# New places in the written order of an attention and feed-forward kernel

## The chip, the cores and the metric

One core of a Trainium2 chip. The metric is the device time of one execution in microseconds. The kernel before was run three times; its median is 1648.62 us (1646.54 to 1649.3). One more execution was taken with the profiler on: it took 1646.02 us, of which 1644.1 us lie between its first and its last instruction (the span of the trace).

## The reference, cut to what matters

```
q   = rms_norm(x @ w_qa.T) @ w_qb.T         # 16 heads, 128 + 64 channels
q_pe = q_pe * cos + rotate_half(q_pe) * sin # the 64 rope channels of each head
c, k_pe = x @ w_kva.T                       # one latent key of 128, one rope key of 64
scores = q_full @ k_full.T * scale          # causal, 2048 x 2048 per head
out = softmax(scores) @ v
x = layernorm(x + out @ w_o.T)
x = layernorm(x + (x @ (weight * scale).T + bias))
```

All is float32. The kernel writes each float32 operand of a matmul as a rounded high part and a rest ("hi" and "lo") and adds the products of the parts.

## The kernel before, in words

A first phase (up to about 150 us) makes keys, values and split weights. Then come attention, the output projection and the feed-forward layer in one long program of single steps.

**Tiles.** The 16 heads are taken in 4 groups of 4. In a group the kernel goes over the 16 query tiles of 128 tokens, two at a time (a pair). One query tile of one group is an iteration `it` (64 of them), and one iteration has one step for each key tile `t` up to the diagonal, `keys(it)` of them. In all there are 544 tiles (iteration, key tile), each 128 keys by 4 heads by 128 queries. The last four iterations have 4, 3, 2 and 1 tiles.

**One tile** goes this way: TensorE makes the scores with five products (L1475) in one of three banks. For `t > 0` ScalarE copies them to a ring of 24 buffers (L1592) and VectorE takes the running maximum (L1849); for `t = 0` VectorE adds the mask (L1839). Later VectorE subtracts the maximum (`shift`, L1880), ScalarE takes the exponential (`exp`, L1597) and rounds it (`hi`, L1604), VectorE sums it (`sum`, L1887), GpSimd forms the rest (`lo`, L1708). TensorE then adds two products with the high part and one with the rest to the bank `OUT` (`values`, L1493, L1494, L1496). `hi` of a tile waits for the value products two tiles before, since `split_p` has two halves.

**One iteration** also has: the maximum over keys (`reduce_max` L1857 on VectorE, `widen_max` L1718 on GpSimd, `fold_max` L1484 on TensorE, `join_max` L1864 and `spread_max` L1872 on VectorE), the same for the sum (`reduce_sum` L1895, `fold_sum` L1505, `spread_sum` L1901 and L1903, `normalise` L1910), `copy_out` (L1610, ScalarE takes `OUT` to `o_sum`; the next iteration's first value product waits for it), `o_hi` (L1616, ScalarE), `o_lo` (L1725, GpSimd), the projection `y` (12 products, L1517; the last four wait for `o_lo`) and `add_y` (L1828). `copy_out` of `it` waits for `o_lo` of `it - 2`.

**One pair** has two projections `q` (18 products each, L1438) with `q_hi` (L1575, ScalarE) and `q_lo` (L1821, VectorE), and one projection `pe` (18 products, L1451). Its result is turned by rope: `rope` on VectorE (three multiplications, L1800 and twice L1804), then on GpSimd one subtraction and one addition (`rotate`, L1681 twice), a rounding on ScalarE (`round_pe`, L1579), the rest on GpSimd (`rest`, L1687), a store to memory and a load in another layout on the SP queue (`store_pe`, `load_pe`).

**The last block** (`ffn`) takes the 16 sums of the last group through layer norm, turn, linear layer and layer norm: units `u` from 0 to 15, with `statistics` (L1929), `centre` (L1623, ScalarE), `invert` (GpSimd), `turn` (L1525, TensorE), `copy_x` (L1640, ScalarE), `rest_x` (L1915, VectorE), `scale` (L1634), `add_bias` (L1747), `linear` (12 products, L1537), `z` (L1946), `z_statistics` (L1952), `z_invert` (GpSimd), `apply` (L1644), `out`.

**What sets the order.** Every engine runs its own steps in the order of one list, `STEPS`. It is made by `plan()`: every step has a place, a number of slots times 13 plus a constant of the table `AT`; the steps are sorted by place; and a step that another one needs (`waits_for`) is put in before it, if it isn't there yet. So a step whose own place is later than that of one that needs it goes where the other goes. Scores of tile number n have place 13 n - 2. The value slot v of a tile is at least 6 slots behind the last scores of its iteration; `shift`, `exp`, `hi`, `sum`, `lo` and `values` are placed from 13 v, the steps of an iteration from its last score slot or its last value slot. Below, 123@10 means slot 123, 10 thirteenths. Three banks `AUX` are shared in turn by `q`, `pe`, `y`, `fold_max`, `fold_sum`, `turn` and `linear`; each waits until the third use before it has been read.

In the kernel before, GpSimd's `rotate` runs at the step `rope`, as does VectorE's `rope`, and the units of the last block have slots 543, 545, ... 567, 570, 572, 574.

Of the kernel before, what the change touches and what calls it, by code (L numbers as in the profile page):

```python
# [742 lines left out]

SPREAD, SCORES_AT, COPIES, SHIFT, EXP, ROUND, VALUES, READ, MAX, USE_AT, FFN_TURN, FFN_LINEAR, FFN = range(13)

W_SLOT = FIRST[N_ITER - 4] + 3
DIRECT = NT - 2
PACE = 2
# [7 lines left out]
def ffn_slots():  # L756

    slots = []
    for u in range(NT):
        ready = last_value(output_of(u)) + (9 if u < DIRECT else 7)  # L760
        if u == 2:
            ready = max(ready, N_TILE)
        slots.append(max(slots[-1] + PACE if slots else W_SLOT + 6, ready))
    return slots
# [5 lines left out]
AT = {'scores': -2, 'max': 7.85, 'shift': -36, 'exp': -22, 'hi': -14, 'sum': -7.75, 'lo': -7.65, 'values': 1, 'reduce_max': 19, 'widen_max': 24, 'fold_max': 38, 'join_max': 46, 'spread_max': -26, 'reduce_sum': 1, 'copy_out': 10, 'fold_sum': 46, 'spread_sum': 38, 'normalise': 33.1, 'o_hi': 51, 'o_lo': 49.25, 'y': 76, 'add_y': 60.15, 'q': 9, 'q_hi': 45.85, 'q_lo': 19.95, 'pe': 6, 'rope': 19.85, 'round_pe': 63, 'store_pe': 58, 'load_pe': 66}  # L770


def timetable():

    for it in range(N_ITER):
        for t in range(keys(it)):
# [3 lines left out]
            for what in ("shift", "exp", "hi", "sum", "lo", "values"):  # L780
                yield 13 * v + AT[what], 0, (what, it, t)
        for what in ("reduce_max", "widen_max", "fold_max", "join_max"):
            yield 13 * last_slot(it) + AT[what], 0, (what, it)
# [3 lines left out]
    for s in range(-2, N_PAIR):  # L787
# [3 lines left out]
        for j, use in enumerate(uses):  # L791
# [7 lines left out]
            if use[0] == "pe":  # L799
                yield 13 * at + AT["rope"], 0, ("rope", s + 2)  # L800
                yield 13 * at + AT["round_pe"], 0, ("round_pe", s + 2)
# [4 lines left out]
def ffn_timetable():  # L806
# [3 lines left out]
    for u in range(NT):  # L810
        n = FFN_SLOT[u]
        if u < DIRECT:
            yield n - 3, FFN, ("in", u)
        yield n + 0, SPREAD, ("statistics", u)
        yield n + 0, ROUND, ("centre", u)
        yield n + 1, FFN, ("invert", u)
        yield n + 1, FFN_TURN, ("turn", u)
        yield n + 2, READ, ("copy_x", u)
        yield n + 2, READ, ("rest_x", u)
        yield n + 2, FFN, ("scale", u)  # L820
        yield n + 3, FFN, ("add_bias", u)
        yield n + 4, FFN_LINEAR, ("linear", u)
        yield n + 5, READ, ("z", u)
        yield n + 5, MAX, ("z_statistics", u)
# [1241 lines left out]
```

## Time and profile before

| | before |
|---|---|
| median of three runs | 1648.62 us (1646.54 to 1649.3) |
| profiled execution | 1646.02 us |
| its span | 1644.1 us |
| outside the span | 1.9 us |
| TensorE busy | 1596.1 us, 97% |
| TensorE weight load busy | 1326.8 us, 81% |
| VectorE busy | 1452.7 us, 88% |
| ScalarE busy | 1117.5 us, 68% |
| GpSimd busy | 992.7 us, 60% |

Shares are of the span. The matmuls of TensorE overlap and their ends are modelled, so "busy" says that one was recorded as under way, not that the array was full. PE is TensorE, PEld its weight load, DVE VectorE, ACT ScalarE, POOL GpSimd.

### The profile page before, as it was taken

The page shows a single profiled execution, that of the slowest core. Times are in us where ns is not written, and L with a number is a line of the kernel's source. Part 1 is how long each engine was busy: PE and PEld are TensorE (multiplying, and loading weights), DVE is VectorE, ACT ScalarE, POOL GpSimd, SP SyncE. Part 2 cuts the span into 40 slices and gives each one's busy share as a digit, 9 for nine tenths or more (in the row PEclk, how much of TensorE's full clock was granted, in tenths as well). Part 3 has the DMA queues.
Part 4 walks back from the last instruction along what each step waited for, and adds up shares of the span by engine and source line. Part 5 has one row for each costly group of instructions (what it writes and reads, how often), then busy time and mean ns, then how long its engine had stood idle before and what let it go on. Part 6 is the DMA issues. An engine that isn't in the chain of part 4 may idle for free.

```text
span 1644.1 us, 26779 instructions
## 1 busy us (share of the span) xinstructions
PE 1596.1 (97%) x8021; PEld 1326.8 (81%) x8021; DVE 1452.7 (88%) x2688; ACT 1117.5 (68%) x2064; POOL 992.7 (60%) x1001
## 2 busy tenths in 40 slices
PE   7999999999999999999999999999999999999887
PEld 5568888878888878878888878788888888888665
DVE  3656899999999999989999899999999999999995
ACT  3554676666777666766777666766767777776674
POOL 4333566665666666666666566566656666666785
PEclk9999999999999999999999999999999999999999
DMA  7994322212321412223212422123123111112322
GB/s 212 364 358 132 115 79 65 91 58 77 130 84 39 142 45 84 71 84 129 84 58 76 122 67 84 39 83 132 60 75 116 46 64 59 52 46 83 106 94 84
DMA packets 112168, 163.93 MB, mean 100 GB/s; under 512 B 13600, under 2 KB 83488, under 8 KB 109984
## 3 DMA queue, kind: packets, MB, share of 16 engines
q1 hardware_dynamic: 105296, 125.86, 23.7%
q10 hardware_dynamic: 1872, 20.19, 3.0%
q0 software_dynamic: 4864, 16.26, 3.0%
q8 instruction: 62, 1.02, 0.3%
q14 instruction: 74, 0.61, 0.1%
HBM read 101.19 MB, written 61.08 MB: 99 GB/s over the span
## 4 chain that ended last, share of the span: by engine, by line
PE 78%; DVE 11%; issue 4%; POOL 3%; DMA 2%; ACT 2%; DVEq 0%; ACTq 0%; SPq 0%; POOLq 0%
PE rows L1475 21%; PE bank L1475 11%; PE rows L1517 8%; PE bank L1496 6%; PE bank L1493 6%; PE bank L1494 6%; PE rows L1438 5%; PE bank L1438 4%; DVE parts L1887 3%; PE bank L1517 2%; DVE top L1849 2%; PE bank L1451 2%; PE rows L392 2%; DMA cq_dram<-cq 2%; DVE bank L1872 1%
## 5 line engine op out<-in xcount | busy, mean ns | idle before, releaser
L1708 POOL TENSOR_TENSOR split_p<-pool,split_p 128x512 fp32r<-128x512 f32 x544 | 702.6, 1297 | 348.3 <-ACT split_p L1604 347.6
L1604 ACT CAST split_p<-pool 128x512 fp32r<-128x512 f32 x544 | 338.4, 622 | 99.7 <-PE bank L1496 70.0
L1887 DVE TRANSPOSE_TENSOR_REDUCE parts<-pool 128x16 f32<-128x512 f32 x544 | 379.3, 697 | 0.2
L1880 DVE TENSOR_TENSOR pool<-bank,pool 128x512 f32<-128x512 f32 x544 | 369.4, 679 | 2.2
L1597 ACT ACTIVATE pool<-pool 128x512 f32<-128x512 f32 x544 | 342.4, 629 | 32.8 <-DVE pool L1880 29.4
L1475 PE MATMUL rows<-q_c,key_c 128*128 128x512 f32 x1089 | 311.4, 394 | 0.0
L1592 ACT COPY pool<-rows 128x512 f32<-128x512 f32 x320 | 186.9, 584 | 123.4 <-PE rows L1475 123.4
L1493 PE MATMUL bank<-split_p,val 128*128 128x512 f32 x544 | 219.6, 404 | 9.9 <-ACT o_sum L1610 9.9
L1475 PEld LDWEIGHTS rows<-q_c,key_c 128*128 128x128 f32 x1089 | 198.2, 189 | 35.7
L1475 PE MATMUL rows<-q_pe,key_pe 128*128 128x512 f32 x726 | 225.1, 391 | 0.0
L1496 PE MATMUL bank<-split_p,val 128*128 128x512 f32 x544 | 214.8, 395 | 2.9 <-POOL split_p L1708 2.6
L1494 PE MATMUL bank<-split_p,val 128*128 128x512 f32 x544 | 213.2, 392 | 0.0
L1849 DVE TENSOR_TENSOR top<-rows,top 128x512 f32<-128x512 f32 x283 | 188.9, 668 | 15.8 <-ACT pool L1592 15.3
L1475 PEld LDWEIGHTS rows<-q_pe,key_pe 128*128 128x128 f32 x726 | 136.6, 188 | 29.6
L1517 PE MATMUL rows<-wo,o_t 128*128 128x512 f32 x600 | 146.6, 392 | 8.2 <-POOL o_t L1725 6.1
L1475 PE MATMUL bank<-q_c,key_c 128*128 128x512 f32 x543 | 154.4, 392 | 0.0
L1517 PEld LDWEIGHTS rows<-wo,o_t 128*128 128x128 f32 x600 | 112.5, 189 | 33.8 <-POOL o_t L1725 7.3
L1592 ACT COPY pool<-bank 128x512 f32<-128x512 f32 x160 | 93.4, 584 | 65.6 <-PE bank L1475 65.6
L1493 PEld LDWEIGHTS bank<-split_p,val 128*128 128x128 f32 x544 | 102.8, 189 | 31.8 <-ACT o_sum L1610 12.6
L1496 PEld LDWEIGHTS bank<-split_p,val 128*128 128x128 f32 x544 | 102.6, 189 | 29.7 <-POOL split_p L1708 8.5
L1494 PEld LDWEIGHTS bank<-split_p,val 128*128 128x128 f32 x544 | 102.9, 189 | 18.8
L1475 PEld LDWEIGHTS bank<-q_c,key_c 128*128 128x128 f32 x543 | 99.4, 189 | 18.6
(200 smaller groups left out, 2378.4 us busy)
## 6 DMA issues: line engine op xcount, KB each, us to landing
q_pe<-pe_dram SPq DMA_DIRECT2D x128, 128.0 KB, 2.6
y_dram<-y SPq DMA_DIRECT2D x62, 256.0 KB, 2.1
cq<-cq_dram SPq DMA_DIRECT2D x19, 768.0 KB, 4.8
y<-y_dram SPq DMA_DIRECT2D x48, 256.0 KB, 3.4
pe_dram<-by_sin SPq DMA_DIRECT2D x32, 256.0 KB, 2.1
pe_dram<-by_cos SPq DMA_DIRECT2D x32, 256.0 KB, 2.1
cq_more<-cq_dram SPq DMA_DIRECT2D x10, 768.0 KB, 5.0
table<-table_dram SPq DMA_DIRECT2D x56, 128.0 KB, 2.7
```

The costliest lines, as they stand in the source:

```text
L1475: mm = pe.matmul(by_head(out), k, q, start=(z == 0), stop=(z == 4))
L1493: pe.matmul(OUT, m.val[:, 0, j, :], split_p[:, n % 2, 0, :], start=(t == 0), stop=False)
L1494: pe.matmul(OUT, m.val[:, 1, j, :], split_p[:, n % 2, 0, :], start=False, stop=False)
L1496: pe.matmul(OUT, m.val[:, 0, j, :], split_p[:, n % 2, 1, :], start=False, stop=(t == keys(it) - 1)).then_inc(values_done, 1)
L1517: mm = pe.matmul(aux(u), o_t[:, a, h * P:h * P + P], m.wo[:, b, h, :], start=(n == 0), stop=(n == 3 * HG - 1))
L1592: nc.scalar.copy(slot(n), SCORES[n % N_SCORES]).then_inc(scores_copied, 1)
L1597: nc.scalar.activation(slot(n), slot(n), ACT.Exp).then_inc(exp_done, 1)
L1604: nc.scalar.copy(split_p[:, n % 2, 0, :], slot(n)).then_inc(p_hi, 1)
L1708: nc.gpsimd.tensor_tensor(split_p[:, n % 2, 1, :], slot(n), stored(split_p[:, n % 2, 0, :]), ALU.subtract).then_inc(p_lo, 1)
L1849: nc.vector.tensor_tensor(out, SCORES[n % N_SCORES], slot(number(it, 0)) if t == 1 else out, ALU.max).then_inc(scores_maxed, 1)
L1880: nc.vector.tensor_tensor(slot(n), MAXES, slot(n), ALU.add).then_inc(shifted, 1)
L1887: nc.vector.tensor_reduce(parts[:, t, :], in_blocks(slot(n)), AX.X, ALU.add, apply_transpose=True).then_inc(summed, 1)
```

## The change

The change alters places and one condition; no instruction is added or taken away.

- `rotate` becomes a step of its own. It needs `rope`, and `round_pe` needs `rotate`. GpSimd runs its subtraction and addition at this step and no longer at `rope`. Its place is `13 * at + 11.9`, where `pe` has `13 * at + 6`; `rope` has 16.85 (it had 19.85).
- The value products of an iteration's first tile have the place 13 v + 10, those of the others 13 v + 1 as before.
- Other places: `shift` -36 to -35, `exp` -22 to -20, `sum` -7.75 to -5.6, `lo` -7.65 to -15.65, `reduce_sum` 1 to -5, `copy_out` 10 to 10.15, `o_hi` 51 to 44, `q_lo` 19.95 to 19.8, `store_pe` 58 to 55.
- The steps of the last block take their places from the same table, in thirteenths, and many move by a few; the block's units get slots 542, 544, ... 572.

```diff
+AT = {'scores': -2, 'max': 7.85, 'shift': -35, 'exp': -20, 'hi': -14, 'sum': -5.6, 'lo': -15.65, 'values': 1, 'reduce_max': 19, 'widen_max': 24, 'fold_max': 38, 'join_max': 46, 'spread_max': -26, 'reduce_sum': -5, 'copy_out': 10.15, 'fold_sum': 46, 'spread_sum': 38, 'normalise': 33.1, 'o_hi': 44, 'o_lo': 49.25, 'y': 76, 'add_y': 60.15, 'q': 9, 'q_hi': 45.85, 'q_lo': 19.8, 'pe': 6, 'rope': 16.85, 'round_pe': 63, 'store_pe': 55, 'load_pe': 66, 'f_in': -27, 'f_statistics': 0, 'f_centre': 6, 'f_invert': 17, 'f_turn': 25, 'f_copy_x': 30, 'f_rest_x': 30.05, 'f_scale': 46, 'f_add_bias': 51, 'f_linear': 63, 'f_z': 70, 'f_z_statistics': 72.85, 'f_z_invert': 85, 'f_apply': 101, 'f_out': 106.05, 'f_ready': -4, 'f_ready_last': 7, 'f_pace': 2, 'f_first': 3, 'w_slot': 5, 'rotate': 11.9, 'values_first': 10.0}
...
-W_SLOT = FIRST[N_ITER - 4] + 3
+W_SLOT = FIRST[N_ITER - 4] + AT["w_slot"]
 DIRECT = NT - 2
-PACE = 2
+PACE = AT["f_pace"]
...
-        ready = last_value(output_of(u)) + (9 if u < DIRECT else 7)
+        ready = last_value(output_of(u)) + (AT["f_ready"] if u < DIRECT else AT["f_ready_last"])
...
-        slots.append(max(slots[-1] + PACE if slots else W_SLOT + 6, ready))
+        slots.append(max(slots[-1] + PACE if slots else W_SLOT + AT["f_first"], ready))
...
-AT = {'scores': -2, 'max': 7.85, 'shift': -36, 'exp': -22, 'hi': -14, 'sum': -7.75, 'lo': -7.65, 'values': 1, 'reduce_max': 19, 'widen_max': 24, 'fold_max': 38, 'join_max': 46, 'spread_max': -26, 'reduce_sum': 1, 'copy_out': 10, 'fold_sum': 46, 'spread_sum': 38, 'normalise': 33.1, 'o_hi': 51, 'o_lo': 49.25, 'y': 76, 'add_y': 60.15, 'q': 9, 'q_hi': 45.85, 'q_lo': 19.95, 'pe': 6, 'rope': 19.85, 'round_pe': 63, 'store_pe': 58, 'load_pe': 66}
...
-            for what in ("shift", "exp", "hi", "sum", "lo", "values"):
+            for what in ("shift", "exp", "hi", "sum", "lo"):
                 yield 13 * v + AT[what], 0, (what, it, t)
+            yield 13 * v + AT["values" if t else "values_first"], 0, ("values", it, t)
...
                 yield 13 * at + AT["rope"], 0, ("rope", s + 2)
+                yield 13 * at + AT["rotate"], 0, ("rotate", s + 2)
...
-        yield n + 0, SPREAD, ("statistics", u)
-        yield n + 0, ROUND, ("centre", u)
...
+        for what in ("in", "statistics", "centre", "invert", "turn", "copy_x", "rest_x", "scale", "add_bias", "linear", "z",
+                     "z_statistics", "z_invert", "apply", "out"):
+            if what != "in" or u < DIRECT:
+                yield n + AT["f_" + what] / 13, 0, (what, u)
...
     elif what == "round_pe":
+        yield ("rotate", it)
+    elif what == "rotate":
         yield ("rope", it)
...
-                elif what == "rope":
+                elif what == "rotate":
                     rotate(*at)
```

## Rows read from the trace of the kernel before

**Rows 1.** The page's first two parts: span, then busy us of each engine.
```profile
span 1644.1 us, 26779 instructions
...
PE 1596.1 (97%) x8021; PEld 1326.8 (81%) x8021; DVE 1452.7 (88%) x2688; ACT 1117.5 (68%) x2064; POOL 992.7 (60%) x1001
```

**Rows 2.** The chain that ended last: start us, us, engine, line.
```profile
168.32 2.27 PE rows L1475 x10
...
255.38 2.15 PE rows L1451 x18
259.62 2.73 PE rows L1517 x12
```

**Rows 3.** Windows: busy us of each engine by stretch, then granted clock and DMA.
```profile
180.00:300.00 120.00, 118.65 (x606) 101.02 (x605) 112.03 (x196) 83.85 (x151) 73.67 (x66) 1.00 0.22 71
300.00:1500.00 1200.00, 1189.45 (x5972) 1009.03 (x5971) 1120.57 (x1948) 850.97 (x1529) 750.40 (x651) 1.00 0.24 79
1528.00:1545.00 17.00, 12.61 (x48) 9.93 (x47) 15.70 (x35) 11.57 (x20) 11.94 (x17) 0.80 0.04 14
1545.00:1590.00 45.00, 39.27 (x180) 30.32 (x179) 42.81 (x96) 31.23 (x55) 40.79 (x70) 1.00 0.31 100
1590.00:1620.00 30.00, 26.67 (x124) 21.50 (x125) 22.69 (x51) 16.26 (x28) 21.62 (x42) 1.00 0.29 97
```

**Rows 4.** TensorE's waits, 180 to 1500 us: total us, times, longest us.
```profile
PE rows L1517 <- POOL o_t L1725: 6.1, 3, 2.0
PE bank L1493 <- ACT o_sum L1610: 4.2, 4, 1.2
PE bank L1496 <- POOL split_p L1708: 1.0, 1, 1.0
```

**Rows 5.** Timeline around 605 us: start, us, engine, line, [idle before].
```profile
606.25 0.50 PE L1493 MATMUL bank<-split_p,val 128*128 128x512 f32 x1 [1.17 <-ACT o_sum L1610]
...
607.05 2.31 PE L1451 MATMUL bank<-cq,wq 128*128 128x256 f32 x18
```

**Rows 6.** Timeline, 342 to 348 us.
```profile
342.58 0.68 DVE L1880 TENSOR_TENSOR pool<-bank,pool 128x512 f32<-128x512 f32 x1
...
343.18 0.70 DVE L1887 TRANSPOSE_TENSOR_REDUCE parts<-pool 128x16 f32<-128x512 f32 x1
...
343.80 0.65 DVE L1800 TENSOR_TENSOR by_cos<-rows,table 128x512 f32<-128x512 f32 x1
...
344.38 0.74 DVE L1804 TENSOR_TENSOR by_sin<-rows,table 128x256 f32<-128x256 f32 x2
...
345.20 1.42 POOL L1681 TENSOR_TENSOR by_cos<-by_cos,by_sin 128x256 f32<-128x256 f32 x2 [5.02 <-DVE by_sin L1804]
...
346.58 1.27 POOL L1725 TENSOR_TENSOR o_t<-o_sum,o_t 128x512 fp32r<-128x512 f32 x1
...
347.90 1.19 PE L1517 MATMUL rows<-wo,o_t 128*128 128x512 f32 x4 [2.03 <-POOL o_t L1725]
```

**Rows 7.** TensorE's waits, 1500 to 1645 us.
```profile
PE bank L1493 <- ACT o_sum L1610: 5.7, 3, 2.2
PE rows L1484 <- DVE x_t L1915: 2.2, 1, 2.2
...
PE rows L1525 <- ACT x_in L1623: 0.3, 1, 0.3
```

**Rows 8.** Timeline of the last block's first and last units.
```profile
1530.40 0.72 ACT L1623 ACTIVATE x_in<-x_in,ffn_small 128x512 f32<-128x512 f32 x1 [1.37 <-DVE ffn_small L1935]
...
1531.03 0.56 ACT L1610 COPY o_sum<-bank 128x512 f32<-128x512 f32 x1
...
1626.05 3.06 PE L1537 MATMUL rows<-w_t,x_t 128*128 128x512 f32 x12 [1.01 <-DVE x_t L1915]
```

**Rows 9.** The page's costliest groups: GpSimd's rest and ScalarE's rounding of one tile.
```profile
L1708 POOL TENSOR_TENSOR split_p<-pool,split_p 128x512 fp32r<-128x512 f32 x544 | 702.6, 1297 | 348.3 <-ACT split_p L1604 347.6
L1604 ACT CAST split_p<-pool 128x512 fp32r<-128x512 f32 x544 | 338.4, 622 | 99.7 <-PE bank L1496 70.0
```

More of the change, by code:

```diff
@@ L811, in ffn_timetable @@
         n = FFN_SLOT[u]
-        if u < DIRECT:
-            yield n - 3, FFN, ("in", u)
-        yield n + 0, SPREAD, ("statistics", u)
-        yield n + 0, ROUND, ("centre", u)
[L816 to L824, printed above, removed]
-        yield n + 6, READ, ("z_invert", u)
-        yield n + 8, COPIES, ("apply", u)
-        yield n + 8, COPIES, ("out", u)
+        for what in ("in", "statistics", "centre", "invert", "turn", "copy_x", "rest_x", "scale", "add_bias", "linear", "z",
+                     "z_statistics", "z_invert", "apply", "out"):
+            if what != "in" or u < DIRECT:
+                yield n + AT["f_" + what] / 13, 0, (what, u)
 def readers(use):
```

## The prediction

> **What bounds the kernel now.** I read the page first. TensorE is busy for 97% of the span, VectorE for 88% [rows 1]. Busy matmul time has modelled ends, so next comes the chain that ended last: back to back, ten score products take 2.27 us, 18 projection products 2.15 us and 12 output products 2.73 us, so a 512-column product costs 0.227 us [rows 2]. Then the windows: from 180 to 1500 us TensorE is busy for 118.65 + 1189.45 = 1308.1 of 1320 us, so it stands idle for 11.9 us there, and VectorE is busy for 112.0 + 1120.6 = 1232.6 us, 93% [rows 3]. TensorE bounds this stretch and VectorE is close behind. TensorE's waits say what the 11.9 us are: 6.1 us in three waits of the output projection for GpSimd's `o_lo`, 4.2 us in four waits of a first value product for `copy_out`, 1.0 us in one wait for `lo` [rows 4]. No wait for a score bank, for `q_lo` or for `fold_max` stands among them. Nothing that only shifts work on another engine inside that stretch can give more than these 11.9 us.
>
> After 1528 us it is another kernel: the last block on top of the last values. VectorE is busy for 15.7 of 17 us, then for 42.8 of 45 us: with 3.5 us idle in 62 it bounds this stretch. TensorE has 10 us idle there. From 1590 us on neither is full (26.7 and 22.7 of 30 us) [rows 3], and short dependencies set the time.
>
> A sentence of the Trainium skill (Perfetto Trace Analysis, Identifying the Most-Contended Engine) speaks against this reading: it has matmul busy time as a bad measure and asks for the share of weight loads, which is 84% here (1009 of 1200 us). By it TensorE would have up to 16% to spare, VectorE would be the bound and the middle's 6.5 us below would be 0. The trace does not bear it out as a gap: ten products in 2.27 us leave no room for an eleventh.
>
> **The change, part by part.** No instruction comes or goes, so all terms are waits.
>
> *First value product.* At 13 v + 10 it passes only what lies between v@1 and v@10 on TensorE: a `pe` (at @6), a `fold_sum` (@7), a `y` (@8, pulled there by `add_y`) or a `q` (@9). In the other slots nothing changes on TensorE. I compared the slots of the first products with those of the projections: 15 of the 64 have one of these in the same slot before the scores end. All four waits of the middle are among them. At 606.25 the product waited 1.17 us for `copy_out` and the 2.31 us of `pe` came right behind [rows 5]; now `pe` goes first and `copy_out` is done before it ends. The next iteration's wait, at 611.5 us, gets a whole `y` of 2.73 us [rows 2] in front. The pattern comes again one group later. Gain: all of 4.2 us [rows 4].
>
> *Rotation.* `rotate` has the place 11.9 and needs `rope` (16.85), so it pulls `rope` up to 11.9: the new 16.85 has no effect. `rope` was at slot r+1@6.85 and is at r@11.9. On VectorE it passes `shift` and `sum` of the next slot. On GpSimd `rotate` keeps its neighbours, since `lo` moves 8 thirteenths up as well and `o_lo` stays. What it buys is seen at 342 us: `shift` 342.58, `sum` 343.18, `rope` 343.80; GpSimd's `rotate` waits 5.02 us for it, holds `o_lo` behind it, and TensorE stands for 2.03 us in the middle of `y` [rows 6]. Passing both gives 343.80 - 342.58 = 1.22 us. But `normalise`, `join_max`, `reduce_max` and `q_lo` now pass `sum` (@7.4 instead of @5.25), and a `normalise` two steps ahead of this `rope` puts that `sum` in its way: 0.62 us back. Net 0.6 us each, and the pattern comes three times: 1.8 of the 6.1 us [rows 4]. Bounds: nothing (if the `sum` costs more) and 3 x 1.22 = 3.7 us.
>
> What waits behind it: `rope` needs the `pe` product, which until now had `shift` and `sum` in front as cover, 0.68 + 0.70 us [rows 6]. Without cover VectorE can stand up to 1.4 us more for each of 30 ropes, at most 41 us of the 87 us that it has idle in the middle. Behind it are `shift`, then `exp`, `hi`, `lo` of a tile whose value slot is three slots on, with at least three score groups of 1.14 us in between, and the maximum that frees a score bank, of which there are three. As no wait for either stands in rows 4, I take 0. The memory side stays: `store_pe` is three thirteenths earlier on SP, passes no transfer, and `load_pe` keeps its place; no wait of TensorE for it is in rows 4. `q_lo` loses up to one `sum` of cover in the same way and is taken at 0.
>
> *`lo`, `hi`, `exp`, `shift`, `sum`, `reduce_sum`, `copy_out`, `o_hi`.* On GpSimd `lo` passes only `widen_max`, which is then 1.30 us later but no longer blocks a `lo` that is ready. `hi` is pulled along and keeps its place behind `copy_out`. `o_hi` and `round_pe` pass `exp`; where `o_hi` has to wait, `exp` is now behind it, about 0.6 us, the length of one rounding [rows 9], which the ring of 24 hides. All 0, except the 1.0 us of the very first values, of which I take half (bounds 0 and 1.0) [rows 4].
>
> *The last block.* Its first slot goes from 543 to 542, its last from 574 to 572. `statistics` and `centre` of unit 0 come a slot earlier, so `centre` (0.72 us at 1530.40) no longer stands in front of `copy_out` (1531.03) [rows 8], for which TensorE waited 2.2 us [rows 7]; and `copy_x` passes the next `centre`, which frees the bank for which `fold_max` waited 2.2 us. VectorE bounds this stretch, though: its idle time up to 1545 us is 1.3 us, and I take that (bounds 0 and the 3.5 us up to 1590 us) [rows 3]. From 1590 to 1620 us a first product that waited for `copy_out` gets `turn` and `y` in front; another (slot 564) loses `linear` in front and keeps only `turn`. Of the two I keep 0.8 us (bounds -1.5 and +3.3, TensorE's idle time there). At the end the distance of units 12 and 13 falls from three slots to two and `copy_x` is ahead of `centre`, so the waits of 1.01 us [rows 8] and 0.3 us before it [rows 7] go: 1.3 us. The chain behind the last `linear` stays. In all 3.4 us.
>
> *The clock.* Between 1528 and 1545 us the granted clock is 0.80 on the mean [rows 3], that is 6.8 us at 1.2 GHz instead of 2.4, which costs TensorE 3.4 us; it fell right after the two waits of 2.2 us. I count 0, as VectorE bounds there. By the Trainium skill (TensorE: Matmul & The Clock Gate, Part 1: The HAM clock gate) the gate follows how busy the array has been of late, and so shorter waits would give these 3.4 us back; the trace agrees in the order of events, though not every such wait of the middle was followed by a fall.
>
> **Sum.** 4.2 + 1.8 + 0.5 + 3.4 = 9.9 us. The profiled execution goes from 1646.0 to 1636.1 us. It lies 2.6 us under the median of the runs, so I forecast 1638.7 us, 0.6% less. A difference of 0.2% (3.3 us) is about what a measurement can tell from none.
>
> **Rivals.**
> - *Only the middle gives (chance 0.17).* The last block is bound by VectorE, its earlier start only queues more work behind the same engine: 6.5 us, 1642.1 us. For it: VectorE is busy for 42.8 of 45 us from 1545 us on [rows 3]. Against it: the loose end behind 1590 us.
> - *More comes back (0.13).* All 11.9 us of the middle, the 3.5 us of VectorE up to 1590 us and 2 us at the end: 17.4 us, 1631.2 us. For it: `o_lo` needs to be only 2 us earlier. Against it: the `sum` in front of `rope`.
> - *No change (0.10).* Uncovered `rope` and `q_lo` stand so long that VectorE, at 93%, becomes the bound of the middle; the 87 us idle are eaten up in places, the gain is paid back: about 1648 us. The skill's sentence above, that TensorE is not the bound, would end here too.
> - *Slower (0.12).* The loop `values` to `hi` to `lo` to `values` two tiles on. Between the end of a first product and the third tile's last product TensorE has two score groups (2.27 us), one tile of products (0.68) and two more (0.46): 3.4 us. The loop needs 0.62 + 1.30 us [rows 9] and three hand-overs of about 0.08 us (`rope` ends at 345.12, `rotate` starts at 345.20 [rows 6]): 2.1 to 2.2 us. A late first product takes away what stood in between as reserve (up to 2.7 us). If two more ScalarE steps of 0.6 us [rows 9] and a `rotate` of 1.42 us [rows 6] all get in the way, it needs 4.7 us: 1.3 us of wait at 15 places, 20 us, less the 9.9 us won: about 1659 us. It decides from 0.66 us a place on. Against it: the engines are free for more than a third of the time.
> - The forecast's own case, 1634 to 1641 us, has 0.48.
>
> **How the numbers follow.** The range takes the forecast, the first two rivals and the edge of the third: 1630 to 1647.5 us leaves out 0.2, most of it on the slow side. Faster by over 0.2% (under 1645.3): 0.48 + 0.17 + 0.13 = 0.78. Within 0.2%: 0.10. Slower: 0.12.
>
> **What would show it.** In the profile after: no wait of L1493 for `copy_out` in the middle; three waits of L1517 for `o_t` near 346, 702 and 1058 us, each of about 1.4 us; TensorE's idle time from 180 to 1500 us about 5.5 us; L1800 right behind a maximum (L1849 or L1839) and waiting for L1451 in more places than now; a granted clock above 0.80 behind 1525 us. The prediction is wrong if TensorE waits at L1496 for `lo` in many places, if L1475 waits for a maximum, or if the stretch behind 1500 us is longer than now.

## The result: 1.1% faster, by more than was forecast

| | before | after |
|---|---|---|
| median of 5 runs each, same chip | 1648.15 us (1646.54 to 1649.3) | 1629.64 us (1629.43 to 1631.57) |
| profiled execution | 1646.02 us | 1629.54 us |
| its span | 1644.1 us | 1627.6 us |

The ratio is 0.9887, with an interval from 0.9876 to 0.9898. The medians are 18.5 us apart, the profiled executions 16.5 us. The forecast was 1638.7 us, 9.9 us less in the profiled execution, with a range from 1630 to 1647.5 us. The time lies 0.4 us outside the range, on the fast side. Of the 2 us between 16.5 and 18.5 the traces show nothing: the median before lies 2.1 us over its profiled execution, that of after 0.1 us. What follows is about the 16.5 us.

Line numbers of the changed kernel are 7 smaller in all steps: L1493 is L1486, L1517 is L1510, L1800 is L1793. The page of the changed kernel, to be held against [rows 1]:

```profile
span 1627.6 us, 26779 instructions
...
PE 1589.9 (98%) x8021; PEld 1326.2 (81%) x8021; DVE 1445.9 (89%) x2688; ACT 1110.2 (68%) x2064; POOL 995.4 (61%) x1001
```

The instructions are the same in number; only waits went. The windows of the changed kernel (columns as in [rows 3]):

```profile
180.00:300.00 120.00, 120.00 (x615) 102.53 (x614) 112.64 (x199) 85.45 (x155) 75.85 (x69) 1.00 0.22 71
300.00:1500.00 1200.00, 1193.97 (x6019) 1016.85 (x6018) 1124.52 (x1962) 850.04 (x1539) 758.50 (x655) 1.00 0.25 80
1518.00:1535.00 17.00, 12.50 (x48) 9.71 (x47) 16.07 (x35) 11.77 (x21) 12.50 (x19) 0.80 0.01 2
1535.00:1580.00 45.00, 40.37 (x188) 31.32 (x187) 42.89 (x97) 34.88 (x60) 41.16 (x72) 1.00 0.31 100
1580.00:1610.00 30.00, 28.41 (x133) 22.82 (x131) 23.43 (x58) 16.20 (x27) 22.15 (x42) 1.00 0.33 106
```

TensorE's idle time between 180 and 1500 us fell from 11.9 us [rows 3] to 6.0 us. The waits of the changed kernel's TensorE in that stretch:

```profile
PE rows L1510 <- POOL o_t L1718: 4.3, 3, 1.4
PE rows L1444 <- DMA wq<-wq_dram: 1.7, 3, 1.0
```

Against [rows 4], all four waits for `copy_out` and the one for `lo` are gone, the three for `o_lo` are 1.4 us long each in place of 2.0, and one kind is new: the projection `pe` waits three times, once for each new group of heads, for its weights (`wq`).

Idle time is not the whole of it. I put the two traces beside each other step by step, with the first scores at zero, and noted at which tile number the changed kernel gets ahead. It is 10.5 us ahead when the scores end:

| where (tile number of the scores) | ahead by, us | in the forecast |
|---|---|---|
| 187 and 188, 323 and 324: first value products | 1.44 + 1.23 + 1.42 + 1.27 = 5.4 | 4.2 |
| 86, 222, 358: `y` behind `o_lo` | 3 x 0.59 = 1.8 | 1.8 |
| 22: the very first values | 1.2 | 0.5 |
| 359: a fall of the granted clock that does not come | 1.55 | 0 |
| 50: a `y` waits less for `o_hi` | 0.5 | 0 |
| four places of a third of a us, others under 0.2 | about 2.4 | 0 |
| 113, 249, 385: `pe` waits for the weights of the next group | -0.47 - 0.62 - 1.17 = -2.3 | 0 |

The last block gives 5.1 us more: the last `linear` starts 15.6 us ahead. The chain behind it is 0.8 us shorter. Of the 5.1 us about 1.5 are won in the first 62 us behind the last scores, where the windows above and [rows 3] end their second stretch (1590 us before, 1580 us after), and 3.6 behind them: counted off instruction by instruction from the last scores, TensorE is 1.5 us ahead at 55 us and 1.9 at 70, VectorE 1.5 at 62 and at 70.

### The profile page after: what moved, and what is told of

It reads as the page before. It is cut to its first block, busy times and chain, and to the rows that moved or that the text cites. A ratio compares the mean times of both kernels' runs of the same rounds, so it can differ in the third digit from the quotient of the medians.

```text
span 1627.6 us, 26779 instructions
## 1 busy us (share of the span) xinstructions
PE 1589.9 (98%) x8021; PEld 1326.2 (81%) x8021; DVE 1445.9 (89%) x2688; ACT 1110.2 (68%) x2064; POOL 995.4 (61%) x1001
## 4 chain that ended last, share of the span: by engine, by line
PE 89%; POOL 3%; DMA 3%; DVE 2%; issue 1%; ACT 1%; DVEq 0%; ACTq 0%; SPq 0%; POOLq 0%
PE rows L1468 25%; PE bank L1468 12%; PE rows L1510 8%; PE bank L1486 7%; PE bank L1489 7%; PE bank L1487 7%; PE rows L1431 5%; PE bank L1431 4%; PE bank L1510 3%; PE bank L1444 2%; PE rows L392 2%; PE rows L1444 2%; DMA wq<-wq_dram 2%; PE rows L1530 1%; POOL split_p L1701 1%
## 5 line engine op out<-in xcount | busy, mean ns | idle before, releaser
L1486 PE MATMUL bank<-split_p,val 128*128 128x512 f32 x544 | 218.5, 402 | 1.3 <-ACT o_sum L1603 1.3
L1510 PE MATMUL rows<-wo,o_t 128*128 128x512 f32 x564 | 136.9, 391 | 4.3 <-POOL o_t L1718 4.3
L1510 PEld LDWEIGHTS rows<-wo,o_t 128*128 128x128 f32 x564 | 105.4, 188 | 27.5 <-POOL o_t L1718 5.6
L1486 PEld LDWEIGHTS bank<-split_p,val 128*128 128x128 f32 x544 | 102.6, 189 | 21.3 <-ACT o_sum L1603 2.2
```

Source lines behind the costliest of these rows:

```text
L1486: pe.matmul(OUT, m.val[:, 0, j, :], split_p[:, n % 2, 0, :], start=(t == 0), stop=False)
L1510: mm = pe.matmul(aux(u), o_t[:, a, h * P:h * P + P], m.wo[:, b, h, :], start=(n == 0), stop=(n == 3 * HG - 1))
```

## What the changed places look like

The timeline of the changed kernel's TensorE at the place of [rows 5]:

```profile
602.35 2.32 PE L1444 MATMUL bank<-cq,wq 128*128 128x256 f32 x18
...
604.50 0.40 PE L1486 MATMUL bank<-split_p,val 128*128 128x512 f32 x1
...
606.48 2.99 PE L1510 MATMUL rows<-wo,o_t 128*128 128x512 f32 x12
609.31 0.39 PE L1486 MATMUL bank<-split_p,val 128*128 128x512 f32 x1
```

`pe` now runs ahead of the first product, which no longer stands, and the next iteration's first product has the whole `y` in front. And at the place of [rows 6]:

```profile
340.67 0.65 DVE L1842 TENSOR_TENSOR top<-bank,top 128x512 f32<-128x512 f32 x1
...
341.25 0.67 DVE L1793 TENSOR_TENSOR by_cos<-rows,table 128x512 f32<-128x512 f32 x1
...
341.85 0.74 DVE L1797 TENSOR_TENSOR by_sin<-rows,table 128x256 f32<-128x256 f32 x2
...
342.66 1.43 POOL L1674 TENSOR_TENSOR by_cos<-by_cos,by_sin 128x256 f32<-128x256 f32 x2 [4.43 <-DVE by_sin L1797]
...
344.06 1.26 POOL L1718 TENSOR_TENSOR o_t<-o_sum,o_t 128x512 fp32r<-128x512 f32 x1
...
345.37 1.19 PE L1510 MATMUL rows<-wo,o_t 128*128 128x512 f32 x4 [1.43 <-POOL o_t L1718]
```

`rope` comes right behind a maximum, as foretold. `rotate` still stands first in GpSimd's queue, 4.43 us in place of 5.02, and still holds `o_lo` behind it: the wait of `y` is 0.6 us shorter, not gone.

At the end of the program TensorE's waits in the changed kernel, from 1500 to 1645 us, are these (before: [rows 7]):

```profile
PE bank L1489 <- POOL split_p L1701: 3.7, 4, 1.2
PE bank L1477 <- POOL wide_max L1711: 2.0, 1, 2.0
PE bank L1510 <- ACT o_t L1609: 1.3, 2, 0.9
PE bank L1486 <- ACT o_sum L1603: 1.3, 1, 1.3
```

`copy_out` cost 5.7 us in three waits and costs 1.3 us in one. The place of the 2.2 us that `fold_max` waited for `rest_x` is taken by 2.0 us for `widen_max`. In the first 62 us behind the last scores TensorE's waits are as long as before, 9.1 us for 9.4. Behind them they fall from 5.3 to 1.8 us. Two that went stood for VectorE's `rest_x`, and VectorE there stood for ScalarE's `copy_x`. From 1590 to 1633 us before:

```profile
PE bank L1537 <- DVE x_t L1915: 1.5, 1, 1.5
PE rows L1537 <- DVE x_t L1915: 1.0, 1, 1.0
```

```profile
DVE x_t L1915 <- ACT x_t L1640: 6.6, 6, 2.0
```

From 1580 to 1618 us after:

```profile
DVE x_t L1908 <- ACT x_t L1633: 1.0, 1, 1.0
```

What moved most is not on TensorE. ScalarE's largest wait between 1515 and 1650 us is `centre` for VectorE's `statistics`; first before, then after:

```profile
ACT x_in L1623 <- DVE ffn_small L1935: 23.3, 15, 4.2
```

```profile
ACT x_in L1616 <- DVE ffn_small L1928: 11.0, 11, 2.0
```

## The experiments

All change only values of the table `AT`. Kernels called "undone" start from the changed kernel, kernels called "alone" from the kernel before, which the new code gives back when every value is set to its old one. "Middle" is what the step by step comparison gives from the first scores to the last, "end" what it gives behind them; both in us of the profiled executions. One execution each stands behind these figures: `u_inv`, which changes nothing in the middle, is 1.5 us later there at its first tile, and such a step is in the middle of `u_tile` and `u_lo` too (1.2 and 1.6 us).

The theories on trial: that each part's gain is its own and adds up, as my sum has it; that the parts carry each other; and, for the end, which part of it gives more than the 3.4 us that I allowed.

### u_first: first value product undone

```diff
-'values_first': 10.0
+'values_first': 1.0
```

> The changed kernel with the first value product back at 13 v + 1. Theory A (first products win what stood before them): the middle loses 5.4 us again, in two steps of 1.4 and 1.3 us near score tiles 187/188 and 323/324, with four waits of L1486 for copy_out. Theory B (the gain at these tiles came from copy_out itself being earlier, through o_hi and lo): the middle loses under 1 us. Whole kernel by A about 1635 us, by B 1630 us; behind 1500 us at most 2 us either way.

1637.3 us, ratio to before 0.9938 (0.9921 to 0.9954). Against the changed kernel 5.65 us later in the middle and 1.4 us at the end. The waits of its TensorE from 150 to 1500 us:

```profile
PE bank L1486 <- ACT o_sum L1603: 5.7, 7, 1.2
```

Here are seven waits where the kernel before has four. At tiles 90, 226 and 362 three new ones of 1.21 us came, at the place behind which the wait for the weights had been: 0.47 + 0.62 + 1.17 us of that are not paid here, since `pe` runs behind the first tile's value products again. The four places of the forecast lose 4.1 us of the 5.4 that they had won; that the middle as a whole comes near the 5.4 us expected is luck (3 x 1.21 lost, 2.3 won back). At 187 and 323 the step was 1.42 and 1.44 us where the waits read were 1.15 and 1.17 us:

```profile
605.30 0.51 PE L1486 MATMUL bank<-split_p,val 128*128 128x512 f32 x1 [1.15 <-ACT o_sum L1603]
```

So a stop costs some 0.27 us more than the idle time on record (1.42 - 1.15).

### u_rope: rope and rotate undone

```diff
-'rope': 16.85, 'rotate': 11.9
+'rope': 19.85, 'rotate': 19.85
```

> The changed kernel with rope and rotate back at 19.85. Theory A (rope passes shift and sum): the three waits for o_lo grow from 1.4 to at least 2.0 us each, the clock falls again near the third one and takes 1.6 us, and the middle loses 3.4 to 5 us: about 1634 us. Theory B (the three steps of 0.6 us came from lo, sum and o_hi): it loses under 1 us. Since sum now stands in front of the maximum and behind normalise, the waits could even be 2.6 us each.

1636.25 us, 0.9929 (0.9912 to 0.9945). Middle 5.1 us later, end 0.2. Its waits in the middle:

```profile
PE rows L1510 <- POOL o_t L1718: 6.1, 3, 2.0
```

The waits for `o_lo` of [rows 4] are back to the number. 1.8 of the 5.1 us are the steps at 86, 222 and 358; the first values cost 0.6, and two falls of the granted clock, at 703 and 1058 us, both right behind a wait for `o_lo`, cost 3.1 us.

### u_tile: shift, exp, sum, lo, the copies, q_lo and store_pe undone

```diff
-'shift': -35, 'exp': -20, 'sum': -5.6, 'lo': -15.65, 'reduce_sum': -5, 'copy_out': 10.15, 'o_hi': 44, 'q_lo': 19.8, 'store_pe': 55
+'shift': -36, 'exp': -22, 'sum': -7.75, 'lo': -7.65, 'reduce_sum': 1, 'copy_out': 10, 'o_hi': 51, 'q_lo': 19.95, 'store_pe': 58
```

> The changed kernel with shift, exp, sum, lo, reduce_sum, copy_out, o_hi, q_lo and store_pe back at their places of before. Theory A (these hardly matter in the middle): it loses the 1.2 us at the very first values and nothing else there, and the o_lo waits get shorter by 0.6 us each since sum hides again in front of normalise: the middle within 1 us of the changed kernel, about 1630 us. Theory B (the earlier lo carries the gain): TensorE waits at L1489 or L1510 in several places, 5 us or more.

1662.04 us, 1.0089 (1.0071 to 1.0107): slower than the kernel before, 32.2 us worse in the middle. I had all of these at 0.

```profile
PE bank L1489 <- POOL split_p L1701: 22.1, 23, 2.9
```

`values` waits 23 times for `lo`. The parts are not independent.

### u_lo: the place of lo alone undone

```diff
-'lo': -15.65
+'lo': -7.65
```

> The changed kernel with lo alone back at -7.65. Undoing nine places cost 32 us. Theory A (it is lo alone: rotate at r@11.9 now stands in front of lo of tile r+2 at r+1@5.35 and holds it): the same, 1660 to 1664 us, with some 20 waits of L1489 for lo, each after a rotate. Theory B (exp, shift and sum carry it): under 10 us, below 1640 us.

1673.55 us, 1.0152 (1.0135 to 1.0169): 49 us worse in the middle, the most costly single value of the change. The profiled execution was the slowest of four; between the medians it is 44 us. First its TensorE's largest wait from 180 to 1500 us, then GpSimd's for `rope` in that stretch:

```profile
PE bank L1489 <- POOL split_p L1701: 32.0, 38, 3.5
```

```profile
POOL by_cos L1674 <- DVE by_sin L1797: 112.0, 29, 6.2
```

One of the 29, in its timeline:

```profile
344.09 0.62 ACT L1597 CAST split_p<-pool 128x512 fp32r<-128x512 f32 x1
...
350.52 1.41 POOL L1674 TENSOR_TENSOR by_cos<-by_cos,by_sin 128x256 f32<-128x256 f32 x2 [6.22 <-DVE by_sin L1797]
...
351.89 1.26 POOL L1701 TENSOR_TENSOR split_p<-pool,split_p 128x512 fp32r<-128x512 f32 x1
...
353.21 0.79 PE L1489 MATMUL bank<-split_p,val 128*128 128x512 f32 x1 [3.46 <-POOL split_p L1701]
353.80 5.32 PE L1510 MATMUL rows<-wo,o_t 128*128 128x512 f32 x12
```

`rotate` stands at the head of GpSimd's queue for 6.22 us, waiting for `rope`. The `lo` behind it, whose `hi` was done at 344.71 us, doesn't run until 351.89 us, although GpSimd has nothing else to do, and `values` stands for 3.46 us. The 12 products of `y` then take 5.32 us in place of 2.73 [rows 2]: they run at the lower clock. In the changed kernel `lo` is placed eight thirteenths up and so ahead of `rotate`.

### a_lo: the place of lo alone, on the kernel before

```diff
-'lo': -7.65
+'lo': -15.65
```

> The kernel before with lo at -15.65 alone, rope and rotate at 19.85. Theory A (lo alone only lifts the first wait and passes widen_max): 1.2 us less near tile 22, the three o_lo waits of 2.0 us as before, 1646 to 1647 us. Theory B (lo ahead of rotate is the gain, and rope's move adds little): 5 us or more less, below 1643 us.

1647.93 us, 1.0 (0.999 to 1.001); the profiled executions differ by 0.1 us. The 1.2 us near tile 22 did not come. The waits of [rows 4] are all there, to the tenth but for 4.1 in place of 4.2. By itself the place of `lo` is worth nothing; it is what makes `rotate` bearable at its new one.

### a_lorope: lo, rope and rotate alone

```diff
-'lo': -7.65, 'rope': 19.85, 'rotate': 19.85
+'lo': -15.65, 'rope': 16.85, 'rotate': 11.9
```

> The kernel before with rope and rotate at 11.9 and lo at -15.65; sum stays at -7.75, in front of normalise. Theory A (lo keeps its neighbours, rope passes shift and sum): the first values win 1.2 us, the three o_lo waits fall by 1.2 us each to about 0.8 us, the fall of the clock at the third one may go (1.6 us): 1641.5 to 1643.5 us. Theory B (sum in front hurts rope): no less than 1646 us.

1638.53 us, 0.9948 (0.9932 to 0.9965): 8.3 us better in the middle, 0.3 worse at the end. `y` wins 1.16 us at each of 86, 222 and 358, twice what it wins in the whole change, because `sum` keeps its old place, ahead of `normalise`:

```profile
PE rows L1510 <- POOL o_t L1718: 2.6, 3, 0.9
```

The first values win 1.16 us, and the fall of the clock behind the third wait (1.56 us) stays away. `pe` waits for no weights, although TensorE is 8.3 us ahead.

### n_sum and u_rest: does the place of sum cost 0.6 us at each o_lo?

```diff
-'sum': -5.6
+'sum': -7.75
```

> The changed kernel with sum back at -7.75, in front of reduce_max, normalise and q_lo. Theory A (sum behind normalise takes back 0.6 of the 1.2 us that rope won): the three o_lo waits fall from 1.4 to 0.8 us, 1.8 us less in the middle, about 1627.8 us. Theory B (sum's place is what lets normalise, copy_out and o_hi come in time elsewhere): new waits for o_t or o_sum, 1630 us or more.

1630.75 us, 0.9898 (0.988 to 0.9916). The three steps are 0.57, 0.59 and 0.60 us better, so the `sum` in front of `rope` costs what I had put down for it (0.62). But 0.63 us is lost at tile 50 and about 0.4 us at each of five other places; in all it is 0.5 us worse in the middle.

`u_rest` sets back all values of `u_tile` except that of `lo`.

> The changed kernel with shift, exp, sum, reduce_sum, copy_out, o_hi, q_lo and store_pe back, and lo left at -15.65. Undoing these and lo cost 32 us, undoing lo alone 49 us. Theory A (all of it is lo behind rotate; the others only shift how much): within 2 us of the changed kernel, 1628 to 1632 us, the o_lo waits 0.6 us shorter each. Theory B (the others carry something of their own): 1634 us or more.

1630.7 us, 0.9895 (0.9878 to 0.9911): 0.7 us worse in the middle, 1.25 in all. So of the 32.2 us of `u_tile`, 31.5 need `lo` to be back as well.

### n_rot: rope at 11.9, rotate late

```diff
-'rope': 16.85, 'rotate': 11.9
+'rope': 11.9, 'rotate': 25.5
```

> The changed kernel with rope at 11.9 and rotate at 25.5, that is behind o_lo where both meet, and behind one lo more. Theory A (rotate, waiting for rope, holds o_lo and with it TensorE): the three waits of 1.4 us of L1510 for o_t go, 4.3 us less in the middle, about 1625.5 us. Theory B (o_lo is late for another reason, or the later rotate holds a lo instead): the waits move to L1489 and the time stays within 1 us of 1629.6 us or gets longer.

1628.2 us (1626.41 to 1628.6), 0.988 (0.9863 to 0.9896). VectorE's `rope` stays where it was pulled; GpSimd's `rotate` goes behind `o_lo`. TensorE's waits from 180 to 1500 us are now

```profile
PE bank L1510 <- ACT o_t L1609: 2.6, 3, 0.9
PE rows L1444 <- DMA wq<-wq_dram: 0.8, 3, 0.3
```

The wait for `o_lo` is gone, 1.7 us better at each of the three places; 1.1 us comes back four tiles on each time, where the next `y` waits for `o_hi`. The middle is 2.6 us better, of which 0.8 us is a shorter wait for weights; 4.3 were expected. In the profiled executions it is 3.1 us better than the changed kernel, in the medians 1.4 us; their intervals overlap.

### n_y: add_y later on top of n_rot

```diff
-'add_y': 60.15
+'add_y': 62.3
```

> The kernel with rotate behind o_lo (1628.2 us) and y two thirteenths later, behind a first value product of the same slot. Theory A (the new 1.1 us at tiles 90, 226 and 362 is y waiting for o_hi): these 3.3 us go and the two steps near 188 and 324, where y covered copy_out, come back with 1.2 us each: 1626.5 to 1627.5 us. Theory B (o_hi is as late for the later y): the waits stay and it is 1629 us or more.

1642.77 us, 0.9965 (0.9947 to 0.9984): 11.7 us worse than `n_rot` in the middle, 3.0 us at tiles 90 and 362 and 1.5 to 1.8 at three others. The waits for `o_hi` did go, but others came in their place. TensorE's largest wait in the middle is now

```profile
PE bank L1486 <- ACT o_sum L1603: 10.0, 5, 2.3
```

These five are first value products that stand for `copy_out`: 2.25 us at tiles 90, 226 and 362, 1.63 us at 188 and 324. At 90 the `y` that had covered the wait runs right behind the product now. The clock falls behind two of the three of 2.25 us. So what the late first product had won is lost at these places, by moving `y` behind it.

### a_first: first value product alone

```diff
-'values_first': 1.0
+'values_first': 10.0
```

> The kernel before with the late first value product alone. Theory A (its worth is independent of the rest): the two pairs of steps near tiles 187 and 323 come, 5.3 us together, the three o_lo waits stay at 2.0 us: about 1642.5 us. Theory B (it needs the earlier lo, since the loop over two tiles loses its reserve): new waits for lo at L1496 take part of it back and it ends above 1645 us.

1647.11 us, 0.9993 (0.9983 to 1.0002). In the middle the four steps come, 1.44 + 0.81 + 1.42 + 0.81 us, and the fall of the clock at 1061 us stays away (1.57 us), but one comes at 350 us instead, behind the first 2.0 us wait for `o_lo`. In all 0.4 to 1.0 us is lost at nine other places; three of them are the waits of `pe` for its weights, which came with this value alone. Net it is 1.4 us better, and the end is 2.4 us worse. Undone from the changed kernel the same value was worth 7.1 us. The loss at the end lies at one place: up to 62 us behind the last scores the two kernels are level, then

```profile
1592.05 4.58 PE L1510 MATMUL rows<-wo,o_t 128*128 128x512 f32 x12 [2.58 <-ACT o_t L1609]
```

`y` has passed a first product that had waited 1.94 us for `copy_out`, and now waits 2.58 us for `o_hi`; its 12 products, in a fall of the clock, take 4.58 us where they took 2.89. That is 2.3 us.

### u_block, a_block, u_blockfirst: the last block's places and slots

```diff
-'f_centre': 6, 'f_invert': 17, 'f_turn': 25, 'f_copy_x': 30, 'f_rest_x': 30.05, 'f_scale': 46, 'f_z': 70, 'f_z_statistics': 72.85, 'f_apply': 101, 'f_out': 106.05, 'f_ready': -4, 'f_first': 3, 'w_slot': 5
+'f_centre': 5, 'f_invert': 25, 'f_turn': 23, 'f_copy_x': 33, 'f_rest_x': 33, 'f_scale': 38, 'f_z': 72, 'f_z_statistics': 73, 'f_apply': 106, 'f_out': 106, 'f_ready': 9, 'f_first': 6, 'w_slot': 3
```

> The changed kernel with the last block's slots and places of before. The middle should be the same to 0.1 us. Behind 1500 us theory A (the last block's places carry the gain of the end): it loses the 5 to 6 us that the changed kernel wins there, about 1635 us, with waits of 2.2 us at the first product of the 60th iteration and at fold_max of the last. Theory B (the end only profits from earlier first products and rounding): it loses under 2 us.

1643.45 us, 0.9971 (0.996 to 0.9982): 13.0 us worse at the end, the middle 0.5 better. My whole term for the block was 3.4 us.

`a_block` has the new values of the block and the old ones of everything else.

> The kernel before with the slots and places of the last block alone. The middle is that of before. Theory A (the last block's places carry the gain of the end by themselves): 5 to 6 us less behind 1528 us, about 1642.5 us. Theory B (they need lo one slot earlier on GpSimd, as undoing them in the changed kernel cost 12 us and not 5): the end wins under 2 us or gets longer, 1646 us or more.

1641.62 us, 0.9964 (0.9951 to 0.9976): 6.0 us better at the end, as much as the whole change. The block gives 6.0 us on the old middle and is worth 13.0 us under the new one. Is that the late first product, which wants the new block? `u_blockfirst` undoes both.

> The changed kernel with slots and places of the last block and the first value product back at 13 v + 1. The middle loses the 5.6 us of the first products. Behind 1515 us the old block cost 12 us with the late first product. Theory A (the late first product lands beside turn and linear of the odd slots and costs 6 us of these 12): only about 6 us remain there, and the whole is about 1643 us, no more than with the late product. Theory B (the two are independent): 12 us remain and the whole is 1648 us or more.

1650.95 us, 1.0017 (1.0005 to 1.0029): 5.6 us worse in the middle and 14.3 at the end. The loss at the end stays with the old block, whether the first product is late or not.

### u_slots, u_places, u_act, u_inv: which part of the block

```diff
-'f_ready': -4, 'f_first': 3, 'w_slot': 5
+'f_ready': 9, 'f_first': 6, 'w_slot': 3
```

> The changed kernel with only the slots of the last block back (first unit at 543, ready + 9, first + 6, w_slot + 3), its places within a unit as changed. Undoing both cost 12 us behind 1515 us. Theory A (the slots carry it: unit 0 a slot earlier is what frees copy_out and the shared bank): 7 us or more of the 12, above 1636 us. Theory B (the places within a unit carry it): under 4 us, below 1634 us.

1630.45 us, 0.9894 (0.9878 to 0.9911): the slots, 542 to 572 in place of 543 to 574, are worth 0.65 us at the end.

`u_places` keeps them and sets back the ten places of `u_block`.

> The changed kernel with only the places within a unit of the last block back (centre 5, invert 25, turn 23, copy_x 33, rest_x 33, scale 38, z 72, z_statistics 73, apply 106), the slots as changed. Theory A (slots): under 4 us, below 1634 us. Theory B (places: copy_x ahead of the next centre, invert ahead of lo): 7 us or more, above 1636 us.

1643.03 us, 0.9971 (0.9961 to 0.998): 12.5 us worse at the end. Of the places, ScalarE's order alone (with `rest_x` on VectorE, which needs `copy_x` and would pull it back up):

```diff
-'f_centre': 6, 'f_copy_x': 30, 'f_rest_x': 30.05
+'f_centre': 5, 'f_copy_x': 33, 'f_rest_x': 33
```

> The changed kernel with centre back at 5 and copy_x and rest_x back at 33: on ScalarE centre(u) is again ahead of exp and of copy_x(u-1). Undoing all places of a unit cost 12.5 us. Theory A (ScalarE standing in centre for VectorE's statistics holds copy_x, and with it rest_x and the shared bank): 8 us or more of them, above 1637 us, with ScalarE's waits for statistics at L1616 up from 9 us to over 20. Theory B (GpSimd's invert is what is late): under 3 us, below 1633 us.

1644.19 us, 0.9974 (0.9961 to 0.9986): 15.6 us worse at the end (its profiled execution is 2.3 us over its median). ScalarE's largest wait there, from 1515 to 1650 us:

```profile
ACT x_in L1616 <- DVE ffn_small L1928: 31.1, 15, 3.6
```

With the old values `centre` of a unit stands ahead of an `exp` that is ready and ahead of the last unit's `copy_x`. ScalarE stands in it for VectorE's statistics for 31.1 us in place of 11.0. My reading of why that reaches the end, which no run took apart further: VectorE meanwhile gets no exponential to sum and no new `x_t`, and comes to the next statistics later. TensorE's clock falls more often as well. The window from 1515 us to the end of each span, first the changed kernel's, then that of `u_act`, shows 0.95 and 0.89 granted; with 1.2 GHz for half of full speed that is 11 us at the lower clock (2 x 0.05 x 112.6) against 29 us (2 x 0.11 x 129.6). The last fall of each lies behind TensorE's last product. Before it stand 6.8 us and 23.9 us, so falls of the clock can make up as much as 8.5 of the 15.6 us (an estimate: half of the 17.1 us); `u_places`, with 13.7 us, has fewer.

```profile
1515.00:1627.60 112.60, 93.88 (x424) 73.74 (x422) 93.92 (x215) 71.65 (x120) 87.47 (x159) 0.95 0.27 91
```

```profile
1515.00:1644.60 129.60, 103.26 (x430) 79.58 (x428) 96.17 (x217) 71.01 (x121) 89.73 (x160) 0.89 0.24 81
```


```diff
-'f_invert': 17
+'f_invert': 25
```

> The changed kernel with invert alone back at 25, behind one more lo on GpSimd. Theory A (ScalarE's order is the cause): under 3 us, below 1633 us. Theory B (invert late makes scale, add_bias and z late): 8 us or more, above 1637 us. If both runs stay low, the cost lies in scale, apply or z together with them.

1630.89 us, 0.9891 (0.9874 to 0.9907): 1.8 us worse at the end.

## Why the prediction was right, and where it was not

**The step that failed.** The terms were idle time as the trace records it, with a ceiling on it: "Nothing that only shifts work on another engine inside that stretch can give more than these 11.9 us." A stop of TensorE turned out to cost more than its recorded idle time, and the fall of the clock behind the third wait for `o_lo` had no term: the middle gave 10.5 us where I had 6.5. At the end the terms behind 1590 us were too small: 0.8 and 1.3 us, and 0 for the chain behind the last `linear`. There the change gives 3.6 us up to the last `linear` and 0.8 behind it, 4.4 where I had 2.1. The mechanisms held; the sizes did not. The last 2.5 us of the miss are no part of the mechanism: I added the 2.6 us by which the median of before lies over its profiled execution, and the changed kernel's lies 0.1 us over its own. Together 4.0 (middle) + 2.5 (end) + 2.5 us are, but for 0.1 us, the 9.1 us between 1638.7 and 1629.6.

**The first products.** Right in mechanism and place; `u_first` brings the waits back. The term was 4.2 us and measured 5.4: I counted the idle time on record, and each of the four stops costs about 0.3 us more than that.

**The rotation.** Right to the tenth: 3 x 0.6 us, `rope` behind a maximum, three waits of 1.4 us left. The two halves of the reckoning hold as well: without the `sum` in the way the gain is 1.16 us a place (`a_lorope`), near the 1.22 of the bound. VectorE did lose cover: it waits for `pe` 13 times, 8.5 us, in place of 3 times, 0.8 us, and for `q_hi` 43.3 us in place of 24.0. None of it reaches TensorE, as I had assumed.

**The step that took the changed rotate at no cost.** I wrote that `rotate` keeps its neighbours on GpSimd since `lo` moves up too. That is so, and it is why the change works; but I gave it one sentence and no price. It is the dearest thing in the change: 49 us if `lo` stays (`u_lo`). No rival had it. The slower rival that I did write, a loop over `values`, `hi` and `lo` that closes at late first products, was not seen: behind the first products TensorE waits for no `lo`.

**The very first values.** 1.2 us, all of the wait and a restart, where I took half. It comes with `lo`, `rope` and `rotate` together (`a_lorope`), not with `lo` alone.

**New waits.** I had none. The weights of `pe` now come late three times, -2.3 us in the step by step comparison. It is the late first product that does it, not a TensorE that comes earlier: at these three places `pe` passes the first tile's three value products, 0.7 us, and meets the load. The waits are there in `a_first`, which is 1.4 us ahead in the middle, and not in `a_lorope`, which is 8.3 us ahead; in `u_first` they are gone. I had looked for DMAs only where the change moves one, and not at what a product that moves up reads.

**The clock.** I counted 0 for the end. That was right, though my own sign, a granted clock above 0.80, did not come: [rows 3] and the window of 1518 to 1535 us above both have 0.80, that is 6.8 us at the lower clock in each. In the middle I had no term, and it was 1.55 us: before, the clock fell for 3.4 us behind the third wait for `o_lo`, of 2.0 us; behind the 1.4 us waits of the changed kernel it never fell. By the Trainium skill (TensorE: Matmul & The Clock Gate, Part 1: The HAM clock gate) the gate follows how busy the array has been of late, so that a shorter wait can spare a fall; here the traces agree for the middle. For the end I cited the same rule for 3.4 us that would come back, and there it gave nothing: two falls of 3.4 us before, one of 6.8 us after.

**The last block.** "VectorE bounds this stretch, though: its idle time up to 1545 us is 1.3 us, and I take that" held up to 1590 us: VectorE's idle time in the 62 us behind the last scores is 3.5 us before and 3.0 after, and about 1.5 us is won. What I had wrong lies behind it. TensorE's waits there fall from 5.3 to 1.8 us. I had a term for the 1.9 us of `copy_out` (0.8) and for the 1.0 and 0.3 us at the end (1.3), and none for the 1.5 us in which a `linear` waited for `rest_x`. VectorE stood 6.6 us for `copy_x` there, 1.0 us after the change: `copy_x` used to run 0.6 to 0.7 us behind the start of the next `centre`, and now runs ahead of it. 15 waits of `centre`, 23.3 us in all, stood in the trace of before, and I read only the first of them, for the `copy_out` behind it. Under the new middle this order is worth most: undoing it alone costs 15.6 us (`u_act`), slots and `invert` 0.65 and 1.8 us. On the old middle only the block as a whole was tried (`a_block`), so that its 6.0 us are the order's is argued from the waits, not shown. Which part took 0.8 us off the chain behind the last `linear` stays open.

**The sum.** Middle 10.5 us where I had 6.5, end 5.9 where I had 3.4. The middle's error is 1.2 of restarts, 0.7 of the first values, 1.6 of clock, 0.5 of `o_hi`, 2.4 in small steps that I can't put to a cause (the four of a third of a us are there in `a_lorope` too), less 2.3 for the weights: 4.1 us. The 11.9 us that I named as a ceiling is not one: 5.9 us of recorded idle time went, and 10.5 us were won. Nor can the terms be summed part by part. Undone one at a time, rotation, block and first product cost 5.3, 12.5 and 7.1 us, 25 us in all, and `lo` 49 more; the change gives 16.5. Alone, `lo` with the rotation gives 8.0 us, the block 6.0, and the first product loses 1.0: 13.0 us.

**TensorE as the bound.** The sentence of the Trainium skill that I had weighed (Perfetto Trace Analysis, Identifying the Most-Contended Engine) would have the middle gain nothing, as weight loads fill 84% of it. It names the share of peak FLOPs beside that of weight loads, which I did not work out. The middle gained 10.5 us when waits of TensorE went, with 1194.0 of 1200 us now busy, and weight loads took 1016.9 us of them. The measurement decides: in this kernel 85% is what a full TensorE shows.

**Open.** Whether `u_act` costs more than `u_places`, which undoes more: 3 us in the profiled executions, with more falls of the clock, but their ratios, 0.9974 and 0.9971, are the same within their intervals; the small steps of the middle; and the 2 us between medians and profiled executions.

## What to carry to other kernels

On an engine that runs a written order, list for every moved step what stands behind it ready to run: an idle engine with a long wait at its head is a closed queue, and the price is paid by the engine that needs what is behind (49 us for one value of a table here). Read the waits of every engine, not only of the one that bounds: 23.3 us of ScalarE's waits in one group was the sign of the gain at the end. And before moving work up on the leading engine, look at what it reads and when that lands: `pe`, 0.7 us earlier in the order, met its weights' load three times and paid 2.3 us.

## What the runs showed of the hardware

- A stop of TensorE costs more than its idle time on record: 1.42 us for 1.15 us, 1.44 us for 1.17 us [rows 5]. A tenth of a us of it can be seen: the first product behind the stop took 0.50 and 0.51 us, without a stop 0.40.
- The granted clock in the middle fell to 1.2 GHz only behind waits of 2.0 us or more, and behind some of these only. For `o_lo`, 2.0 us: one of three before, in `a_lo`, `a_first` and `a_block`, two of three in `u_rope`. For `copy_out`, 2.25 us: two of three in `n_y`. For `lo`, 2.85 us: two of three in `u_tile`; 3.5 us: three of three in `u_lo`, 6.8 us at the lower clock each. None followed the 1.63 us waits of `n_y` or the 1.4 us waits of the changed kernel. A fall of 3.4 us cost about 1.6 us.
- The weights for `pe` (2304 KB) land 8.7 us after their load is issued, 8.9 us after the change (medians of three). Before the change that is 2.7 us ahead of the scores of tile 113, and `pe` starts 2.15 us ahead of them; after it 3.1 us ahead, and `pe`, which waits, starts 2.9 us ahead.
